# An AdaLN transformer block with a ternary feed-forward: reordering the opening

## The reference, cut to what matters

```python
ada = cond @ ada_w + ada_b                       # shift1, scale1, gate1, shift2, scale2, gate2
x1  = ln(x) * (1 + scale1) + shift1              # per sequence
qkv = x1 @ qkv_w + qkv_b                         # 16 heads of 128
attn = softmax(q @ k.T / sqrt(128)) @ v          # inside each sequence of 32
x = x + gate1 * (attn @ out_w + out_b)
x = x + gate2 * (gelu((ln(x) * (1 + scale2) + shift2) @ ffn_w1 + b1) @ ffn_w2 + b2)
return x_in + bit_ffn(x)                         # rms norm, 8-bit activations, ternary weights
```

## Time and profile before

| | us |
|---|---|
| median of 3 runs | 351.39 (350.51 to 352.80) |
| profiled execution, its own time | 352.6 |
| its span, first to last instruction | 350.8 |
| TensorE busy in the span | 336.2 (96%) |
| VectorE busy | 218.7 (62%) |
| ScalarE busy | 174.8 (50%) |
| GpSimd busy | 129.1 (37%) |

### The profile page before, as it was taken

How to read it: one execution, slowest core, us unless ns; L and a number is a source line. 1 busy time by engine, 2 the same in 40 slices (tenths; PEclk the granted TensorE clock), 3 DMA queues, 4 the chain that set the end, 5 groups by cost and what they waited for, 6 DMA issues and landing times. The chain is left out here.

```text
span 350.8 us, 9793 instructions
## 1 busy us (share of the span) xinstructions
PE 336.2 (96%) x4187; PEld 302.4 (86%) x4187; DVE 218.7 (62%) x425; ACT 174.8 (50%) x343; POOL 129.1 (37%) x115
## 2 busy tenths in 40 slices
PE   8899999999999999999999999999999999999766
PEld 7788899898998989899898998789998789997345
DVE  3689745826758953504366065689276599775884
ACT  1134435554416365356334545579163755467492
POOL 2686303200843662565120530225230233116680
PEclk9999999999999999999999999999999999999887
DMA  7995920320036540110020010200000200200001
GB/s 236 348 258 160 325 110 2 92 62 2 2 120 182 154 153 30 64 30 2 2 63 4 1 32 2 60 3 2 32 32 2 60 4 4 78 14 0 2 0 60
DMA packets 20834, 24.41 MB, mean 70 GB/s; under 512 B 1780, under 2 KB 18328, under 8 KB 20792
## 3 DMA queue, kind: packets, MB, share of 16 engines
q1 hardware_dynamic: 20416, 23.50, 21.3%
q10 hardware_dynamic: 376, 0.30, 0.3%
HBM read 22.68 MB, written 1.11 MB: 68 GB/s over the span
## 5 line engine op out<-in xcount | busy, mean ns | idle before, releaser
L1556 ACT ACTIVATE q_t<-proj_banks,bias_cols 128x256 f32<-128x256 f32 x64 | 30.6, 478 | 67.4 <-PE proj_banks L552 67.4
L552 PE MATMUL proj_banks<-x_hi,w_hi 128*128 128x256 f32 x256 | 53.6, 291 | 1.5 <-issue 0.9
L552 PE MATMUL proj_banks<-x_lo,w_hi 128*128 128x256 f32 x256 | 51.6, 283 | 0.6 <-DVE x_lo L1087 0.6
L552 PE MATMUL proj_banks<-x_hi,w_lo 128*128 128x256 f32 x256 | 51.5, 283 | 0.0
L552 PEld LDWEIGHTS proj_banks<-x_hi,w_hi 128*128 128x128 f32 x256 | 40.1, 191 | 2.8 <-issue 1.9
L552 PEld LDWEIGHTS proj_banks<-x_lo,w_hi 128*128 128x128 f32 x256 | 39.8, 191 | 0.8 <-DVE x_lo L1087 0.8
L1150 DVE TENSOR_TENSOR v_sb<-proj_banks,bv_row 128x512 f32<-128x512 f32 x32 | 21.7, 685 | 29.6 <-PE wide_banks L630 29.6
L552 PEld LDWEIGHTS proj_banks<-x_hi,w_lo 128*128 128x128 f32 x256 | 39.8, 191 | 0.0
L630 PEld LDWEIGHTS att_banks<-probs_t,v_sb 32*128 32x128 f32 x512 | 29.8, 186 | 5.5 <-issue 5.4
L630 PE MATMUL att_banks<-probs_t,v_sb 32*128 32x32 f32 x512 | 31.6, 272 | 0.0
L1556 ACT ACTIVATE k_t<-proj_banks,bias_cols 128x256 f32<-128x256 f32 x64 | 30.2, 471 | 0.0
(11 more groups left out here) (284 smaller groups left out, 788.2 us busy)
## 6 DMA issues: line engine op xcount, KB each, us to landing
stage<-in_L_cond_qkv_w SPq DMA_DIRECT2D x16, 256.0 KB, 3.8
gate<-gate_rows_scratch SPq DMA_DIRECT2D x48, 64.0 KB, 2.4
stage<-in_L_cond_qkv_w SPq DMA_DIRECT2D x4, 512.0 KB, 5.0
stage<-in_L_cond_out_w SPq DMA_DIRECT2D x4, 512.0 KB, 4.2
work<-in_L_ffn_w SPq DMA_DIRECT2D x2, 1024.0 KB, 8.9
xin<-in_x SPq DMA_DIRECT2D x7, 256.0 KB, 3.2
bv_row<-in_L_cond_qkv_b SPq DMA_DIRECT2D x4, 256.0 KB, 5.1
work<-in_L_cond_ada_w SPq DMA_DIRECT2D x1, 1024.0 KB, 9.7
```

The costliest lines, as they stand in the source:

```text
L552: mm = pe.matmul(dst, l, r, start=start and i == 0, stop=stop and i == len(seq) - 1)
L1556: act.activation(dst[:, h, :], proj_bank[h % 2][:, s * QT:(s + 1) * QT], ACT.Identity, bias=bias_cols[:, c:c + 1]).then_inc(qk_kept, 1)
```

## The change

Six things are done to the opening.

1. SP loads the scale columns of `ada_w` ahead of the shift columns.
2. TensorE turns the biases first, then multiplies the scale columns, turns the rows of quarter 0, and only then multiplies the shift columns (into `out_bank`). VectorE scales with the first result, and adds with the second when it comes (`opening_x`). Six of `keep_running`'s matmuls behind the turn become three.
3. The high parts of the weights of groups 0 and 1 are copied by ScalarE (`high_qk`, `high_v`), and no longer by VectorE.
4. The low parts of the q and k weights of group 0 are subtracted by VectorE (`low_qk`), and no longer by GpSimd.
5. The first two heads of unit 0 are multiplied together (`opening_qk`): the high x high passes of both, then both with the low weights, then both with the low x1, where before one head came after the other.
6. In units 1 and 3, `x_norm` of quarters 2 and 3 stands behind `softmax_shift` and no longer ahead of it.

```diff
-            for i in range(2):
+            for i in (1, 0):
                 sp.dma_start(ada_w_sb[:, :, i * D:(i + 1) * D], ...).then_inc(ada1_in[i], 16)
...
+            def opening_qk():
+                def passes(h, left, right, start=False, stop=False):
+                    for s in range(2):
+                        for k in range(KD):
+                            c0 = (s * KD + k) * HW + h * P
+                            mm = pe.matmul(proj_bank[h][:, s * QT:(s + 1) * QT], left[0][:, c0:c0 + P], right[:, 0, k, :],
+                                           start=start and s == 0 and k == 0, stop=stop and s == 1 and k == KD - 1)
+                    return mm
+                heads = range(HG // HALVES)
+                pe.wait_ge(x1_hi_made, 1)
+                pe.wait_ge(qk_hi, 1)
+                for h in heads:
+                    passes(h, w_hi, x1_hi, start=True)
+                pe.wait_ge(qk_lo, 1)
+                for h in heads:
+                    passes(h, w_lo, x1_hi)
+                pe.wait_ge(x1_lo_made, 1)
+                for h in heads:
+                    passes(h, w_hi, x1_lo, stop=True).then_inc(projected, 1)
...
             keep_running(3)
-            pe.wait_ge(cols_made, 1)
-            ada_cols(proj_bank[1], 0, ada1_in)
             pe.wait_ge(bias_in, 48)
             pe.transpose(att_bank[0][:, 0:NBIAS], bias_rows, ident[0:NBIAS, 0:NBIAS]).then_inc(turned0, 1)
+            pe.wait_ge(cols_made, 1)
+            ada_cols(proj_bank[1], 0, ada1_in, (1,))
             x_turn(0)
-            keep_running(6)
+            ada_cols(out_bank, 0, ada1_in, (0,))
+            keep_running(3)
+            opening_qk()
...
+            def low_qk(c):
+                s = slice(c * CH, (c + 1) * CH)
+                dve.wait_ge(qk_hi, c + 1)
+                dve.tensor_tensor(w_lo[0][:, s], stage[:, s], w_hi[0][:, s].bitcast(F32), ALU.subtract).then_inc(qk_lo, 1)
+            def opening_x():
...
+                dve.tensor_tensor(d4, s4, conditions(KD, 0), ALU.mult).then_inc(x1_scaled, 1)
+                ada_part(0, 2, out_bank, False)
...
+                dve.tensor_tensor(hi..., d4, conditions(0, 0), ALU.add).then_inc(x1_hi_made, 1)
+                low_qk(0)
...
+                dve.tensor_tensor(d4, d4, conditions(0, 0), ALU.add).then_inc(x1_ready, 1)
+                dve.tensor_tensor(x1_lo[:, 0], x2, hi.bitcast(F32), ALU.subtract).then_inc(x1_lo_made, 1)
+                low_qk(1)
...
                 attention_tail(u)
-                if u in (1, 3):
-                    x_norm(u // 2 + 2)
...
                 if u > 0:
                     softmax_shift(u)
-                if u == 6:
+                if u in (1, 3):
+                    x_norm(u // 2 + 2)
...
             load_table(ACT.Exp)
+            for c in range(HALVES):
+                high_qk(0, c)
+            high_v(0)
             act.wait_ge(cols_made, 2)
...
+                if u == 1:
+                    high_v(1)
...
                 if u == 0:
+                    for c in range(HALVES):
+                        high_qk(1, c)
                     high_wo(0)
...
             x_rstd(0)
-            low_half(0, 0)
-            low_half(0, 1)
+            pool.wait_ge(qk_lo, HALVES)
             low_v(0)
```

More of the change, by code:

```diff
@@ L647, in out_proj, with ada_cols @@
                            late=("lhsT", (at_lo_made, 2 * u + 2)) if t == 0 else None).then_inc(out_mm, 1)
-            def ada_cols(dst, first, loaded):
-                for j in range(2 * KD):
-                    if j % KD == 0:
-                        pe.wait_ge(loaded[j // KD], 16)
-                    for k in range(KD):
-                        c0 = first + j * P
-                        mm = pe.matmul(dst[:, j * NB:(j + 1) * NB], ada_w_sb[:, k, c0:c0 + P], cond_t[:, k, :],
-                                       start=(k == 0), stop=(k == KD - 1))
+            def ada_cols(dst, first, loaded, parts):
+                for i in parts:
+                    pe.wait_ge(loaded[i], 16)
+                    for j in range(i * KD, (i + 1) * KD):
+                        for k in range(KD):
+                            c0 = first + j * P
+                            mm = pe.matmul(dst[:, j * NB:(j + 1) * NB], ada_w_sb[:, k, c0:c0 + P], cond_t[:, k, :],
+                                           start=(k == 0), stop=(k == KD - 1))
                 mm.then_inc(ada_mm, 1)
@@ L867, in _ @@
                 if u == 0:
-                    ada_cols(side, 3 * D, [ada2_in, ada2_in])
+                    ada_cols(side, 3 * D, [ada2_in, ada2_in], range(2))
                 if u in (2, 4, 5):
@@ L1416, in _ @@
                     softmax_shift(u)
-                if u == 6:
+                if u in (1, 3):
+                    x_norm(u // 2 + 2)
+                elif u == 6:
                     tern_ratio()
@@ L1572, in acc_keep, with high_qk, high_v @@
                 act.copy(xa[:, :, :], out_bank[:, :].rearrange("p (i d) -> p i d", i=2)).then_inc(acc_kept, 1)
+            def high_qk(g, c):
+                s = slice(c * CH, (c + 1) * CH)
+                act.wait_ge(qkw_in[c], 32 * (g + 1))
+                act.copy(w_hi[g][:, s], stage[:, s]).then_inc(qk_hi, 1)
+            def high_v(g):
+                act.wait_ge(vw_in, 16 * (g + 1))
+                act.copy(w_hi[g][:, SLOT:], stage[:, SLOT:WO]).then_inc(vw_hi, 1)
             def high_wo(g):
```

65 lines of the change are left out of this document (33 added, 32 removed).

## The result

| us | before | changed |
|---|---|---|
| median of 7 runs | 351.39 (350.38 to 352.80) | 349.26 (348.45 to 349.69) |
| profiled execution, its own time | 352.6 | 348.54 |
| its span | 350.8 | 346.7 |
| mean granted clock of TensorE in it | 0.985 | 0.995 |

The ratio is 0.9919, with a 95% interval from 0.9890 to 0.9948. The change wins 2.1 us where 0.74 was forecast.

The account below looks back on a forecast made before the run. TensorE, busy 96% of the span, was taken as the bound, with only its few early waits worth removing. Terms +0.33 - 0.25 - 0.82 gave -0.74 us, so 351.39 became 350.65 us, range 349.2 to 352.6.

Parts of the forecast that it names:

- third head of unit 0: TensorE's third head in unit 0: starts at 16.81 us instead of 16.48, released by ScalarE, a loss of 0.33.
- scores of unit 0: TensorE's scores in unit 0: VectorE's v additions no longer late, as quarter 1's normalisation takes 0.73 us; gain 0.25.
- gates of unit 0: TensorE's work behind the scores of unit 0: the prediction gave it no term in its sum.
- end of unit 1, to the mark in unit 2: Wait ahead of unit 2 goes as the softmax shift comes first: gain 0.82 us. Mark: second matmul of unit 2's second v product.
- sum at the mark: All terms up to unit 2 together: +0.33 - 0.25 - 0.82 = -0.74 us.
- The start of the bias turn: TensorE's first work in the opening: bias rows land at 6.05 (bounds 5.9 and 6.3), plus 0.25, so start at 6.30 us.
- The clock's rise: TensorE going from 1.2 to 2.4 GHz in the opening: expected at about 14.7 us, called the largest open price.
- the overlap of scaling and shift half: VectorE scales while TensorE multiplies the shift columns, ahead of the first product: wins 0.7 us.
- (a): Rival: TensorE stays at 1.2 GHz through the opening; with a rise at 20 us, +1.2 us, median 352.6; chance 12%.
- (b): Rival: the clock is up at once, by about 12 us; -1.23 us, median 350.2; chance 12%.
- (c): Rival: the bias rows' landing decides the first product; landing at 6.8 us gives no change, 351.4; chance 9%.
- (d): Rival: the end's half-clock stretch gains or loses more than the opening, 349.0 or 352.3 us; chance 13%, both ways alike.

Follow-up runs that it names:

- norm_alone: The kernel before with only step 6, `x_norm` behind `softmax_shift` in units 1 and 3: median 350.41 us, ratio 0.9961 to the kernel before.
- norm_ahead_again: The changed kernel with step 6 undone, `x_norm` again ahead of `softmax_shift` in units 1 and 3: median 350.31 us, ratio 0.9955 to the kernel before.
- parts_as_before: The changed kernel without steps 3 and 4, so VectorE casts high parts and GpSimd subtracts low ones: median 351.06 us, ratio 0.9982 to the kernel before.
- before_late8: The kernel before with eight `keep_running` calls (1.76 us) added between units 0 and 1: median 352.92 us, ratio 1.0040 to the kernel before.
- before_tail_warm: The kernel before with more `keep_running` calls in TensorE's waits near the end: median 349.87 us, ratio 0.9953 to the kernel before.
- changed_again: The changed kernel run once more with nothing edited, beside the second round of experiments: median 348.50 us, ratio 0.9896 to the kernel before.

## Why the prediction was right in direction and wrong in size

| step | forecast us | measured us |
|---|---|---|
| third head of unit 0 | +0.33 | -0.61 |
| scores of unit 0 | -0.25 | -0.39 |
| gates of unit 0 | none | -0.24 |
| end of unit 1, to the mark in unit 2 | -0.82 | -0.92 |
| sum at the mark | -0.74 | -2.16 |

The mechanism was right at three of the four places: what the third head waits for, the scores, and the end of unit 1. The sum was short by 1.42 us, in the terms below: 0.51 for the start of the bias turn, 0.14 and 0.08 behind it, 0.21 for the clock, 0.24 for the gates, 0.14 for the scores and 0.10 for the end of unit 1.

- **The start of the bias turn is the term that failed most.** The prediction took 6.05 for the landing from the last packets and added 0.25 for the wait to become a matmul: 6.30. Measured: 5.75 and 0.04, so 5.79. The 0.25 came from no row, and is plainly wrong: in all nine profiles where TensorE stood waiting for these rows the turn started 0.04 to 0.05 behind the landing. The 6.05 was right for its trace (6.03); the landing moves from one execution to the next (5.4 to 6.5 over the profiles), so that 0.30 of the miss is chance. The first product came at 11.36, 0.73 before the forecast's 12.09; 0.51 of that is this term. Another 0.14 lies in the steps behind it, and 0.08 between the high part and the product. That turned "the result is later" into "earlier".
- **The clock's rise** was taken at 14.7 and came at 13.2 here. From the first product to the third head that made 4.51 for 4.72, so 0.21. It was said to be the largest open price, and it is: over the profiles with the changed opening it came between 5 us (with a fall after it) and 14.5, and the third head between 14.42 and 16.52. A forecast from one trace couldn't have met that but by luck.
- **The gates** weren't in the sum: a term put at nothing without a reason. The prediction stopped at the scores and priced the v additions, but TensorE's next work, the gates, waited for VectorE too, for the two additions of the ada columns behind these: 0.77 from the start of the scores before, 0.55 now. By the starts of unit 1 it is 0.24.
- **Right:** the overlap of scaling and shift half; the high part at 0.69 and quarter 1's normalisation at 0.74; the low part at 1.22 (1.23 forecast, from two other sizes on a line); ScalarE as the third head's releaser; no new wait in unit 1; and the end of unit 1, where unit 2's first product gains 0.85 for 0.82, by norm_alone 0.85, by norm_ahead_again 0.84. The high part's 0.69 for 0.86 is right by what the other profiles show, though parts_as_before had the 0.69 with GpSimd at work. In the four profiles in which the high part started before GpSimd's subtraction was over, it ended 0.55 behind it, and took 0.69, 0.86, 1.03 and 1.69 (parts_as_before, before, before_late8, before_tail_warm); so what moving that subtraction gives hangs on when the weights land. The Trainium skill, "SBUF — State Buffer", section "SBUF: two separate sides", gives a reason: a VectorE instruction with two SBUF inputs (against a GpSimd instruction that reads SBUF), or in a mode that uses two ports, and a GpSimd instruction exclude one another. The rows agree: quarter 1's normalisation took 2.81 against 0.74 with GpSimd's work moved away, and 2.80 again once it was put back.
- **The rivals.** (a) and (b), the clock in the opening, both occurred in part in other executions, but their sums rest on the first product's wrong start. (c), late biases: norm_ahead_again shows 0.44 of it. (d) was right in kind for the profiled pair: the end took 1.9 us less, near the 1.7 of its estimate. By the medians the whole change gave 2.1 us in the first measurement and 3.4 in the second (changed_again), of which the opening is 1.8 to 2.0. What is left for the end, 0.1 to 1.6, can't be told from nothing, since the intervals of the two ratios overlap (0.9890 to 0.9948, 0.9869 to 0.9924).
- **Luck.** That the time lay inside the stated range is no merit: it did so by 0.06 us, and the second measurement, 348.50, lies outside it.

What stays open: whether the changed kernel's 13 executions at 0.990 or 0.995, where the kernel before ranges wider, are more than chance, what a delay costs beyond its length, and what moves the clock's rise in the opening between 5 and 14.5 us. With the end's clock held up both kernels have the same tail (18.9), so there the whole difference is the opening's.

## What to carry to other kernels

Where an engine's first work waits for a small transfer, read when the same rows landed in several executions before pricing the wait: half a us decided the sign of a term here, and 0.2 of it was a price that no row showed. When a slow engine is relieved, list all that wait for it in the next stage and not only the next one: the weights' copies were worth 0.8 us through the scores and gates of unit 0, and nothing at the product that they feed. Read the opening's clock in several executions as well: an edit of 1 us can't be sized from one profile if the same program's third head moves by 2. And if TensorE's granted clock falls in a kernel's last, thinly filled stretch, try filling its waits with matmuls that compute nothing: three changed numbers gave 1.7 us on the kernel before, nearly as much as the whole reordering.

## What the runs showed of the hardware

- The time of the kernel before followed its mean granted clock. 35 executions on one chip had spans of 347.7 us at 1.000, 348.5 to 348.9 at 0.995, 348.7 to 350.0 at 0.990, 349.7 to 351.3 at 0.985 and 351.3 to 351.9 at 0.976. That spread of 4 us is larger than the change. In the changed kernel the order didn't hold: with the end filled the shortest span had 0.995 (344.2), and 345.5 to 346.4 had 1.000.
- The same 104 matmuls and their waits took 18.9 us at a clock of 1.00, 20.1 at 0.92 and 22.0 at 0.77. With the filled waits it was 18.9 in each of four profiles, of both kernels.
- The clock could be up at 5.0 to 5.4 us, down again at 8.5 to 11.9, and up for good at 12 or 18.7, in kernels whose instructions up to there were as in others that rose once. With the changed opening, unedited, the first rises were at 5.2, 5.4, 13.0, 13.0, 13.2, 13.5 and 14.5; with the old one, four, at 5.0, 11.3, 11.7 and 14.0. The Trainium skill, "TensorE: Matmul & The Clock Gate", section "What you observe", says of back-to-back matmuls that the rise varies by half a us from run to run; in this opening, which has idle stretches, it varied by several, and the measurement decides.
- Small transfers of 68 rows for the biases had landed, in the profiles, between 5.4 and 6.5 us, though they had been issued by 2.6. TensorE's matmul started 0.04 to 0.05 us behind the landing that it waited for.
- A VectorE addition of 128x512 from two SBUF inputs, which alone took 0.69 us, took up to 1.69 when GpSimd's subtraction was under way: it ended 0.55 us behind the end of that, in all four profiles in which the two met.
